# Involution on one Trainium2 core: GpSimd's ten taps move from the last to taps 7 to 16, and the logits are laid out pixel by pixel

## The chip, the cores and the metric

The program runs on one core of a Trainium2 chip. The metric is the device time of one execution in microseconds. The core has TensorE (matmuls, PE in the profile), VectorE (DVE), ScalarE (ACT), GpSimd (POOL) and SyncE (SP, which here only issues DMAs). Each engine runs its own list of instructions in order; they meet through semaphores.

## The reference, cut to what matters

A convolution-like layer (involution), then attention, then a routed feed-forward layer. The change touches the involution alone:

```
x1, x2, x3 = conv1x1(x, w1), conv1x1(x, w2), conv1x1(x, w3)       # 32, 32 and 256 channels, 56 x 56 pixels, 4 images
feat = concat([x1 - unfold_7x7(x2), p - unfold_7x7(p)])           # 49 taps per pixel, reflected borders
y = relu(bn(feat)); y = relu(bn(conv1x1(y, cw1)))
wgt = softmax(conv1x1(y, cw2, cb2), axis=taps)                    # 32 groups x 49 taps per pixel
out = sum over the 49 taps of  patch(x3, tap) * wgt[group, tap]   # 8 channels share a group
```

## The kernel before

The kernel has four stages, one after the other: projection (`project_stage`), involution (`conv_stage`), attention and feed-forward. The involution cuts the 56 rows of the image into 14 blocks of 4 rows. The 128 partitions are 4 images by 32 groups; a block has 224 pixels (`PW`).

For a block a there are two halves of work. The logits half: for each of the 7 rows i of the 7x7 window GpSimd forms `z(a, i)` = x1 - shifted x2 (7 taps at once), ScalarE applies a relu, and TensorE and ScalarE run the chain, two steps c per row i, 14 in all: `first` (matmul, cw1 and position features), `second` of ScalarE (relu), `second` of TensorE (matmul, cw2), `third` (ScalarE writes the logits `lg`). VectorE keeps a running maximum over taps (`rowmax`, L655) and folds it into `mx` (L659 to L665). The weighting half: GpSimd subtracts the maximum, row by row (`shift`, L466, `lg` to `ex`), ScalarE takes the exponent in place (`expo`, L548) and copies the weights of two taps to PSUM (`weights`) and into the products' ninth plane (`denominators`), VectorE multiplies two taps at once with the window of x3 (`pair`, L679), and TensorE adds the products of all taps into PSUM by an identity matmul (`add`, L742, nine planes: eight channels and the sum of the weights). The last ten taps (`OWN` = 10) are multiplied by GpSimd instead (`own`, L483), which also copies the weight into the ninth plane (L484). At the end VectorE divides (`divide`, L638 and L642) into `osb`, and SP stores `osb` to DRAM (`store`, L507).

The two halves of neighbouring blocks overlap. A slot handles the logits of block a and the weighting of block b = a - 1, in 20 units u, one per tap pair. The order on each engine is written out: `CH_AT` puts chain step c at unit c + 1, `MAX_AT` the maxima at units 5, 7, ... 17 (the fold at 17), `EXP_NEXT` and `FIRST_AT` the exponents of rows 2 to 6 and the relus, `OWN_AT` the units in which TensorE adds GpSimd's taps, and `POOL_ORDER` GpSimd's own sequence: z0, z1, shift 2, 3, z2, shift 4, 5, z3, shift 6, z4, z5, own 0, 1, z6, own 2 to 8; then shift 0 and shift 1 of the next block, then own 9. Shift 0 and 1 need the new `mx`, so they tie one slot to the next. VectorE divides block b - 1 in unit 1 of the slot.

The waits that matter here. `z(i)` needs the chain steps of row i - 2. SP issues the position features of row i after the chain steps of row i - 2 (four DMAs), and the store of block b - 1 right after those of row 3, so after chain step 3 (unit 4). GpSimd's taps alternate between two buffers: `own_a`, and `own_b`, which is the memory of `osb`; so `own(1)` waits until the store of the previous block has landed (L477). There are two product buffers, so pair p waits until pair p - 2 is summed.

## Time and profile before

| | us |
|---|---|
| median of 3 runs | 3883.24 (3878.19 to 3886.63) |
| the profiled execution's own time | 3877.12 |
| its span in the trace | 3875.3 |
| first and last division of the involution (starts) | 352.6 and 1714.1 |

The profile is one execution. A busy time is the union of an engine's instructions over the span or over a stretch. "Idle before" is the idle time of the engine just ahead of an instruction, with what ended it. PEclk is TensorE's granted clock as a share of the full 2.4 GHz. A matmul in float32 shows as two records, so one tap's 16 matmuls are 32 records.

### The profile page before, as it was taken

The numbers are of one execution on the slowest core, as the hardware profiler recorded it, in microseconds if no ns is written. First come the engines' busy times: TensorE is split into PE (matmuls) and PEld (weight loads), VectorE is DVE, ScalarE is ACT, GpSimd is POOL, SyncE is SP. The second block draws the span as 40 slices with busy tenths as digits, with TensorE's granted clock in tenths as the row PEclk, the third lists the DMA queues.
The fourth block names the chain that finished last, engine by engine and source line by source line (L and its number), as shares of the span: only waits on it lengthen the run. The fifth ranks groups of instructions, "written<-read, shape, count | busy, mean of one in ns | idle before, by whom it ended". The sixth has DMA issues, their size and how long they took to land. (4 is left out here: it accounts for less than half of the span.)

```text
span 3875.3 us, 102116 instructions
## 1 busy us (share of the span) xinstructions
PE 3125.9 (81%) x42750; PEld 1556.8 (40%) x42750; DVE 2569.3 (66%) x2229; ACT 2013.4 (52%) x3476; POOL 1962.9 (51%) x1032
## 2 busy tenths in 40 slices
PE   4767777878787777757989999999999994588797
PEld 1224444434343444324343524353344432355465
DVE  6259999999999999977456735664565545444212
ACT  1275556666666555524756575557556653334120
POOL 1269888988899898854140504051223401422422
PEclk9888899999999888888999999999999997788898
DMA  5611111111111111120121102111111103333443
GB/s 202 196 56 56 47 57 49 43 59 59 57 57 55 55 55 47 31 70 26 26 60 48 46 11 58 58 26 26 53 48 26 26 20 100 127 122 124 126 128 117
DMA packets 169451, 257.40 MB, mean 66 GB/s; under 512 B 81600, under 2 KB 128616, under 8 KB 165944
## 3 DMA queue, kind: packets, MB, share of 16 engines
q1 hardware_dynamic: 157120, 219.82, 18.8%
q0 software_dynamic: 11392, 31.02, 2.5%
q8 instruction: 359, 5.88, 0.6%
q14 instruction: 76, 0.62, 0.1%
q10 hardware_dynamic: 504, 0.05, 0.0%
HBM read 152.29 MB, written 79.27 MB: 60 GB/s over the span
## 5 line engine op out<-in xcount | busy, mean ns | idle before, releaser
L742 PE MATMUL ps<-prod,ident 32*32 32x504 f32 x17472 | 935.8, 646 | 257.2 <-issue 180.5
L679 DVE TENSOR_TENSOR prod<-ps,win 128x3584 f32<-128x3584 f32 x280 | 1054.5, 3790 | 99.7 <-PE ps L742 56.1
L1065 POOL TENSOR_TENSOR phk<-kv 128x768 f32<-128x768 f32 (+1 forms) x200 | 349.2, 1751 | 964.6 <-ACT kv L1173 902.6
L742 PEld LDWEIGHTS ps<-prod,ident 32*32 32x32 f32 x17472 | 380.5, 108 | 464.5 <-issue 413.9
L1217 ACT ACTIVATE phq<-ps 128x896 f32<-128x896 f32 x448 | 384.3, 917 | 212.7 <-PE ps L1501 211.8
L457 POOL TENSOR_TENSOR y<-a1w,x2w 128x1568 f32<-128x1568 f32 x98 | 345.9, 3538 | 137.5 <-PE ps L723 120.4
L466 POOL TENSOR_TENSOR ex<-lg,mx 128x1568 f32<-128x1568 f32 x98 | 345.1, 3541 | 16.0 <-DVE mx L665 15.8
L1501 PE MATMUL ps<-qst,sel 96*128 96x448 bf16 x1120 | 293.0, 365 | 25.1 <-ACT phq L1217 7.0
L561 ACT ACTIVATE ps<-ex 128x448 f32<-128x448 f32 x280 | 148.4, 533 | 293.9 <-DVE prod L679 293.9
L1316 DVE TENSOR_TENSOR phk<-ps,kv 128x1280 f32<-128x1280 f32 (+1 forms) x200 | 295.4, 1480 | 0.7 <-ACT ps L1177 0.7
L483 POOL TENSOR_TENSOR osb<-ex,win 128x1792 f32<-128x1792 f32 x70 | 270.2, 3859 | 28.5 <-PE ps L742 28.5
L483 POOL TENSOR_TENSOR own_a<-ex,win 128x1792 f32<-128x1792 f32 x70 | 262.3, 3747 | 43.4 <-issue 21.7
L585 ACT ACTIVATE y<-ps,u2c,s2c 128x784 f32<-128x784 f32 x189 | 189.1, 1000 | 169.2 <-PE ps L723 168.8
L1532 PE MATMUL ps<-phq,snt 128*32 128x448 f32 (+1 forms) x2240 | 273.2, 560 | 3.9 <-ACT phq L1219 3.9
L718 PE MATMUL ps<-y,cw1bd 32*32 32x392 f32 x3136 | 214.9, 514 | 52.1 <-DMA cwp<-cw1p 25.9
L1764 POOL DMA_INDIRECT yg<-rows_dram,dest x100 | 95.3, 953 | 313.2 <-DMA rows_dram<-yt 280.0
L2159 PE MATMUL ps<-xct,w_s 128*128 128x392 f32 x512 | 204.2, 547 | 61.6 <-ACT hid L1880 37.7
L1479 PE MATMUL ps<-phk,kv 128*32 128x288 f32 (+3 forms) x3200 | 237.4, 413 | 15.6 <-ACT phk L1182 9.0
L1458 PE MATMUL ps<-wkv_s,xn 128*128 128x256 f32 (+1 forms) x800 | 224.8, 406 | 9.5 <-ACT kv L1178 5.1
L592 ACT ACTIVATE lg<-ps,par 128x784 f32<-128x784 f32 x196 | 179.1, 914 | 81.6 <-PE ps L734 81.6
L1374 DVE TENSOR_TENSOR at<-ps,rd 128x448 f32<-128x448 f32 x56 | 35.0, 625 | 279.3 <-PE ps L1532 279.3
L734 PE MATMUL ps<-y,cw2bd 32*32 32x392 f32 x3024 | 191.8, 519 | 24.6 <-ACT y L585 21.4
(261 smaller groups left out, 5283.7 us busy)
## 6 DMA issues: line engine op xcount, KB each, us to landing
win<-planes SPq DMA_DIRECT2D x14, 2480.0 KB, 9.0
pf<-pf_dram SPq DMA_DIRECT2D x392, 55.1 KB
qst<-qsp SPq DMA_DIRECT2D x96, 196.0 KB, 4.7
planes<-stage SPq DMA_DIRECT2D x7, 1984.0 KB, 7.0
xs<-in_x SPq DMA_DIRECT2D x8, 1568.0 KB, 21.4
conv_dram<-osb SPq DMA_DIRECT2D x56, 224.0 KB, 4.8
t<-in_x SPq DMA_DIRECT2D x28, 448.0 KB, 4.0
xn<-conv_dram SPq DMA_DIRECT2D x28, 448.0 KB, 6.3
```

What stands on the lines that cost most here:

```text
L457: pool.tensor_tensor(o, x1, x2, ALU.subtract).then_inc(z_ready, 1)
L466: pool.tensor_tensor(ex[:, i], lg[:, i], m, ALU.subtract).then_inc(shifted, 1)
L483: pool.tensor_tensor(o[:, :, 0:SHARE], w.unsqueeze(2).broadcast_to([P, RW, SHARE, W]), xw, ALU.mult).then_inc(own_ready, 1)
L679: v.tensor_tensor(o, w, xw, ALU.mult).then_inc(prod_ready, 1)
L742: mm = pe.matmul(ps[32 * h:32 * h + 32, 4 + r, 0:DENC], diag(ident, r), x[32 * r:32 * r + 32, h].rearrange("p s w -> p (s w)"), start=begi ...
L1065: pool.tensor_tensor(phk[j % 2][0:r, :, ROT_V * DH:FLIN].rearrange("p h (r i) -> p h r i", i=DH), ki.unsqueeze(2).broadcast_to([r, HPG, RO ...
L1217: act.activation(dst, src, ACT.Square).then_inc(phq_done, 1)
L1316: v.tensor_tensor(phk[j % 2][0:r, :, DH:ROT_V * DH].rearrange("p h (r i) -> p h r i", i=DH), same.unsqueeze(2).broadcast_to([r, HPG, ROT_V ...
L1458: mm = pe.matmul(ps[0:r, 4 + j % 2, 0:HPG * DH + P], xn[:, k, j * P:j * P + r], wkv_s[:, k, hg, :], start=(k == 0), stop=(k == CH - 1))
L1479: pe.matmul(ps[DH * h:DH * h + DH, f, 0:hi - lo], kv[j % 3][0:r, v0:v0 + DH], phk[j % 2][0:r, h, lo:hi], start=(j == 0), stop=(j == NT - 1))
L1501: mm = pe.matmul(ps[:, h, 0:CT], sel[:, f, :], qst[:, h, ch(c)], start=True, stop=True)
L1532: mm = pe.matmul(ps[DH * h:DH * h + DH, out_bank(hg, c), 0:CT], snt[0:kr, f, DH * h:DH * h + DH], phq[k % 2][0:kr, h, :], start=(f == 0), ...
```

## The change

GpSimd's ten taps are no longer 39 to 48 but 7 to 16 (row 1 of the window and three of row 2), and they are spread over the slot instead of standing at its end. VectorE's pairs are formed of the remaining 39 taps. The denominator copy of GpSimd's taps goes to ScalarE. The logits and the running maximum are stored pixel by pixel, with the 7 taps of a window row next to each other: VectorE takes each row's maximum with a tensor_reduce over these 7 (instead of a running two-input maximum), and a second tensor_reduce over the 7 rows gives `mx` (instead of three folding steps). GpSimd's shift reads this layout and writes `ex` as before. Waits are made finer, the exponent of row 1 moves behind the first two `weights`, and the last of VectorE's pairs, not the last own tap, now ends the sum. In the projection stage two semaphores become one.

```diff
 OWN = 10
+OWN_TAPS = list(range(K7, K7 + OWN))
+PAIR_TAPS = [t for t in range(TAPS) if t not in OWN_TAPS]
...
-EXP_NOW = {FOLD_AT + 1: 0, FOLD_AT + 2: 1}
-EXP_NEXT = {2: 2, 4: 3, 6: 4, 8: 5, 10: 6}
-FIRST_AT = [0] + [2 * i - 1 for i in range(1, K7)]
-POOL_ORDER = [("z", 0), ("z", 1), ("shift", 2), ("shift", 3), ("z", 2), ("shift", 4), ("shift", 5), ("z", 3), ("shift", 6),
-              ("z", 4), ("z", 5), ("own", 0), ("own", 1), ("z", 6)] + [("own", k) for k in range(2, OWN - 1)]
-OWN_AT = [NPAIR_D - OWN + k for k in range(OWN)]
+EXP_FIRST_AT = FOLD_AT + 1
+EXP_NEXT = {0: 2, 2: 3, 5: 4, 8: 5, 11: 6}
+FIRST_AT = [2 * i for i in range(K7)]
+POOL_ORDER = [("z", 0), ("z", 1), ("shift", 2), ("shift", 3), ("own", 0), ("z", 2), ("own", 1), ("shift", 4), ("z", 3), ("own", 2),
+              ("shift", 5), ("z", 4), ("own", 3), ("shift", 6), ("own", 4), ("z", 5), ("own", 5), ("z", 6), ("own", 6), ("own", 7),
+              ("own", 8)]
+OWN_AT = [3, 5, 7, 9, 11, 13, 14, 15, 16, 18]
+def pairs_of_row(i):
+    return max([p // 2 + 1 for p, t in enumerate(PAIR_TAPS) if t // K7 == i], default=0)
+def own_to_row(i):
+    return sum(t // K7 <= i for t in OWN_TAPS)
...
-        lg = sb("lg", [P, K7, RW, K7, W])
+        lg = sb("lg", [P, K7, PW, K7])
-        run = sb("run", [P, RW, K7, W])
+        run = sb("run", [P, PW, K7])
...
             def shift(b, i):
                 pool.wait_ge(maxed, b.n + 1)
                 if not b.early(1):
-                    pool.wait_ge(den_in, NPAIR_D * (b.n - 1) + FREE_ROW_PAIRS if i < FREE_ROW else NPAIR_D * b.n)
-                if i == FREE_ROW and not b.early(1):
-                    pool.wait_ge(own_ready, 2 * OWN * b.n)
+                    if pairs_of_row(i):
+                        pool.wait_ge(den_in, NPAIR_D * (b.n - 1) + pairs_of_row(i))
+                    if own_to_row(i):
+                        pool.wait_ge(own_den, OWN * (b.n - 1) + own_to_row(i))
+                        pool.wait_ge(own_ready, OWN * (b.n - 1) + own_to_row(i))
+                l = lg[:, i].rearrange("p (h w) j -> p h j w", w=W)
-                pool.tensor_tensor(ex[:, i], lg[:, i], m, ALU.subtract).then_inc(shifted, 1)
+                pool.tensor_tensor(ex[:, i], l, m, ALU.subtract).then_inc(shifted, 1)
...
                 if k == 1 and not b.early(1):
                     pool.wait_ge(stored, 16 * RW * b.n)
-                if k >= 2:
-                    pool.wait_ge(own_used, (OWN - 1) * b.n + k - 1)
+                if k >= 2 or not b.early(1):
+                    pool.wait_ge(own_used, OWN * b.n + k - 1)
...
-                pool.tensor_copy(o[:, :, SHARE], w).then_inc(own_ready, 1)
...
                 if a:
                     shift(a, 0)
-                    shift(a, 1)
                 if b:
                     own(b, OWN - 1)
+                if a:
+                    shift(a, 1)
...
+            def own_denominators(b, k):
+                i, j = OWN_TAPS[k] // K7, OWN_TAPS[k] % K7
+                act.wait_ge(exped, b.q(i) + 1)
+                if k == 1 and not b.early(1):
+                    act.wait_ge(stored, 16 * RW * b.n)
+                if k >= 2 or not b.early(1):
+                    act.wait_ge(own_used, OWN * b.n + k - 1)
+                act.activation(own_buf[k % 2][:, :, SHARE], ex[:, i, :, j, :], ACT.Copy).then_inc(own_den, 1)
...
-                    act.activation(lg[:, i, h:h + 2].rearrange("p h j w -> p h (j w)"), ps[:, k:k + 2, 0:CW],
-                                   ACT.Identity, bias=par[:, CB2:CB2 + 1]).then_inc(logit, 1)
+                    act.activation(lg[:, i, h * W:(h + 2) * W].rearrange("p (h w) j -> p h j w", w=W),
+                                   ps[:, k:k + 2, 0:CW].rearrange("p h (j w) -> p h j w", w=W), ACT.Identity, bias=par[:, CB2:CB2 + 1]).then_inc(logit, 1)
...
-                    if a and u in EXP_NOW:
-                        expo(a, EXP_NOW[u])
+                    if a and u == EXP_FIRST_AT:
+                        expo(a, 0)
                     if a and u in FIRST_AT:
                         first(FIRST_AT.index(u))
+                    if b and u + 1 in OWN_AT:
+                        own_denominators(b, OWN_AT.index(u + 1))
                 if a:
                     weights(a, 0)
                     weights(a, 1)
                     denominators(a, 0)
+                    expo(a, 1)
...
-                    v.tensor_tensor(run[:], lg[:, i], lg[:, 0] if i == 1 else run[:], ALU.max).then_inc(ranmax, 1)
+                    v.tensor_reduce(run[:, :, i], lg[:, i], AX.X, ALU.max).then_inc(ranmax, 1)
...
-                    v.tensor_tensor(run[:, :, 0:3], run[:, :, 0:3], run[:, :, 4:7], ALU.max).then_inc(ranmax, 1)
-                    v.wait_ge(ranmax, NMAX * a.n + K7)
-                    v.tensor_tensor(run[:, :, 0:2], run[:, :, 0:2], run[:, :, 2:4], ALU.max).then_inc(ranmax, 1)
-                    v.wait_ge(ranmax, NMAX * a.n + K7 + 1)
+                    v.wait_ge(ranmax, K7 * (a.n + 1))
                     if b:
                         v.wait_ge(shifted, K7 * a.n)
-                    v.tensor_tensor(mx[:].rearrange("p (h w) -> p h w", w=W), run[:, :, 0], run[:, :, 1], ALU.max).then_inc(maxed, 1)
...
-                    await_ge(own_ready, 2 * (OWN * b.n + k + 1))
-                    mm = add(own_buf[k % 2], False, k == OWN - 1)
-                    if k < OWN - 1:
-                        mm.then_inc(own_used, 1)
-                    else:
-                        mm.then_inc(acc_done, 1)
+                    pe.wait_ge(own_den, OWN * b.n + k + 1)
+                    await_ge(own_ready, OWN * b.n + k + 1)
+                    add(own_buf[k % 2], False, False).then_inc(own_used, 1)
```

The waits of SP's `load_win` and of VectorE's `divide` on the end of the whole sum become waits on the last pair's sum.

## Rows read from the trace of the kernel before

**Rows 1.** Section 1 of the page: busy time of each engine, share of the span, instructions.
```profile
PE 3125.9 (81%) x42750; PEld 1556.8 (40%) x42750; DVE 2569.3 (66%) x2229; ACT 2013.4 (52%) x3476; POOL 1962.9 (51%) x1032
```

**Rows 2.** Busy time by stretch: one slot, mx to mx; columns in the first line.
```profile
core 0: us, PE busy (x) PEld busy (x) DVE busy (x) ACT busy (x) POOL busy (x), PEclk, DMA share, GB/s
...
549.80:656.10 106.30, 85.52 (x2128) 43.72 (x2128) 99.63 (x31) 64.77 (x82) 94.82 (x35) 0.92 0.18 54
```

**Rows 3.** The instruction that writes mx: count, ns min/median/max, first and last start.
```profile
L665 DVE TENSOR_TENSOR mx<-run x14: 391/393/440, 235.5 to 1617.6; 128x224 f32<-128x224 f32 x14
```

**Rows 4.** Groups of VectorE in that slot: busy us, mean ns, idle before.
```profile
L679 DVE TENSOR_TENSOR prod<-ps,win 128x3584 f32<-128x3584 f32 (+1 forms) x20 | 75.4, 3790 | 6.4 <-PE ps L742 3.3 <-ACT ps L561 2.9
L655 DVE TENSOR_TENSOR run<-lg,run 128x1568 f32<-128x1568 f32 x5 | 13.9, 2779 | 0.0
L661 DVE TENSOR_TENSOR run<-run 128x448 f32<-128x448 f32 x1 | 4.0, 3966 | 0.0
...
L659 DVE TENSOR_TENSOR run<-run 128x672 f32<-128x672 f32 x1 | 0.9, 907 | 0.0
```

**Rows 5.** The running maximum, all slots; then VectorE's timeline at the stage's end.
```profile
L655 DVE TENSOR_TENSOR run<-lg,run x70: 1773/2300/5244, 209.0 to 1609.9; 128x1568 f32<-128x1568 f32 x70
...
1714.07 1.56 DVE L638 RECIPROCAL run<-ps 128x224 f32<-128x224 f32 x1 [4.66 <-PE ps L742]
```

**Rows 6.** VectorE's reductions: ns min/median/max, elements out and in.
```profile
L1977 DVE TENSOR_REDUCE count<-mask x32: 543/544/547, 3263.1 to 3598.8; 128x15 f32<-128x375 bf16 x32
...
L1984 DVE TENSOR_REDUCE dig<-hits x32: 168/169/170, 3264.6 to 3601.6; 128x1 f32<-128x15 f32 x32
...
L1330 DVE TENSOR_REDUCE corr<-sn x8: 954/957/967, 1860.5 to 3109.1; 128x32 f32<-128x480 f32 x8
```

**Rows 7.** GpSimd's instructions by line: ns min/median/max.
```profile
L466 POOL TENSOR_TENSOR ex<-lg,mx x98: 3483/3539/3595, 236.0 to 1646.9; 128x1568 f32<-128x1568 f32 x98
...
L457 POOL TENSOR_TENSOR y<-a1w,x2w x98: 3222/3274/4403, 178.6 to 1581.3; 128x1568 f32<-128x1568 f32 x98
...
L483 POOL TENSOR_TENSOR own_a<-ex,win x70: 3689/3722/3895, 290.8 to 1704.6; 128x1792 f32<-128x1792 f32 x70
...
L484 POOL COPY own_a<-ex x70: 359/382/1962, 294.4 to 1708.3; 128x224 f32<-128x224 f32 x70
...
L168 POOL COPY stage<-stage x42: 317/483/491, 69.7 to 161.2; 128x72 f32<-128x72 f32 x42
...
L1041 POOL MEMSET eps<- x1: 117/117/117, 1726.8 to 1726.8; 128x1 f32 x1
```

**Rows 8.** Timelines of TensorE (chain step 3) and SP, and landing of one store.
```profile
587.79 0.81 PE L718 MATMUL ps<-y,cw1bd 32*32 32x392 f32 x9
...
588.44 0.40 PE L723 MATMUL ps<-pf,cwp 18*32 18x392 bf16 x8
...
589.03 3.19 SPq L535 DMA_DIRECT2D pf<-pf_dram  x4
592.49 4.12 SPq L507 DMA_DIRECT2D conv_dram<-osb  x4
...
DMA to landing us min/median/max: 3.7/4.8/5.7
```

**Rows 9.** Timeline of ScalarE in one unit; then its group of 224-element copies.
```profile
588.94 0.99 ACT L585 ACTIVATE y<-ps,u2c,s2c 128x784 f32<-128x784 f32 x1
...
591.34 0.91 ACT L592 ACTIVATE lg<-ps,par 128x784 f32<-128x784 f32 x1 [0.48 <-PE ps L734]
592.15 1.50 ACT L548 ACTIVATE ex<-ex 128x1568 f32<-128x1568 f32 x1
...
L568 ACT ACTIVATE prod<-ex 128x224 f32<-128x224 f32 x14 | 5.5, 391 | 42.2 <-PE ps L742 42.2
```

**Rows 10.** Timeline of TensorE: most of an own tap, and a gap.
```profile
619.13 1.37 PE L742 MATMUL ps<-own_a,ident 32*32 32x504 f32 x28
...
624.76 2.06 PE L742 MATMUL ps<-prod,ident 32*32 32x504 f32 x32 [3.25 <-issue]
```

More of the change, by code:

```diff
@@ L390, in conv_stage @@
         cwp = sb("cwp32", [P, REL], BF16)
-        run = sb("run", [P, RW, K7, W])
+        run = sb("run", [P, PW, K7])
         mx = sb("mx", [P, PW])
-        den = run[:].rearrange("p h j w -> p (h j w)")[:, 0:B * W].rearrange("p (b w) -> p b w", w=W)
+        den = run[:].rearrange("p x i -> p (x i)")[:, 0:B * W].rearrange("p (b w) -> p b w", w=W)
         cw1 = sb("cw1bd", [P, REL])
@@ L473, in own @@
                 pool.wait_ge(exped, b.q(i) + 1)
-                if k == 0 and not b.early(1):
-                    pool.wait_ge(acc_done, b.n)
                 if k == 1 and not b.early(1):
                     pool.wait_ge(stored, 16 * RW * b.n)
-                if k >= 2:
-                    pool.wait_ge(own_used, (OWN - 1) * b.n + k - 1)
+                if k >= 2 or not b.early(1):
+                    pool.wait_ge(own_used, OWN * b.n + k - 1)
                 w = ex[:, i, :, j, :]
@@ L517, in load_win @@
                 if not a.early(2):
-                    sp.wait_ge(acc_done, a.n - 1)
+                    sp.wait_ge(summed, NPAIR_D * (a.n - 1))
                 sp.dma_start(win[a.par][:], planes[:, bass.ds(a.n * RW, RW + K7 - 1)]).then_inc(win_in[a.par], 16)
@@ L551, in tap_pair @@
                 n = min(2, ND - 2 * p)
-                at = [t // K7 * K7 * PW + t % K7 * W for t in range(2 * p, 2 * p + n)]
+                at = [t // K7 * K7 * PW + t % K7 * W for t in PAIR_TAPS[2 * p:2 * p + n]]
                 e = ex[:]
@@ L636, in divide @@
                 acc = ps[:, 4:8]
-                v.wait_ge(acc_done, m + 1)
+                v.wait_ge(summed, NPAIR_D * (m + 1))
                 v.reciprocal(den, acc[:, :, SHARE * W:DENC]).then_inc(divided, 1)
@@ L647, in rowmax @@
                 def rowmax(i):
-                    if i == 0:
-                        return
                     v.wait_ge(logit, a.g(2 * i + 2))
-                    if i == 1 and b and not b.early(1):
+                    if i == 0 and b and not b.early(1):
                         v.wait_ge(divided, 2 * b.n)
-                    if i > 1:
-                        v.wait_ge(ranmax, NMAX * a.n + i - 1)
-                    v.tensor_tensor(run[:], lg[:, i], lg[:, 0] if i == 1 else run[:], ALU.max).then_inc(ranmax, 1)
+                    v.tensor_reduce(run[:, :, i], lg[:, i], AX.X, ALU.max).then_inc(ranmax, 1)
                 def fold():
-                    v.wait_ge(ranmax, NMAX * a.n + K7 - 1)
-                    v.tensor_tensor(run[:, :, 0:3], run[:, :, 0:3], run[:, :, 4:7], ALU.max).then_inc(ranmax, 1)
-                    v.wait_ge(ranmax, NMAX * a.n + K7)
-                    v.tensor_tensor(run[:, :, 0:2], run[:, :, 0:2], run[:, :, 2:4], ALU.max).then_inc(ranmax, 1)
-                    v.wait_ge(ranmax, NMAX * a.n + K7 + 1)
+                    v.wait_ge(ranmax, K7 * (a.n + 1))
                     if b:
                         v.wait_ge(shifted, K7 * a.n)
-                    v.tensor_tensor(mx[:].rearrange("p (h w) -> p h w", w=W), run[:, :, 0], run[:, :, 1], ALU.max).then_inc(maxed, 1)
+                    v.tensor_reduce(mx[:], run[:], AX.X, ALU.max).then_inc(maxed, 1)
                 def pair(p):
@@ L674, in pair @@
                     w = ps[:, 2 + p % 2, 0:n * PW].rearrange("p (n h w) -> p n h w", h=RW, w=W).unsqueeze(3).broadcast_to([P, n, RW, SHARE, W])
-                    at = [t // K7 * SHARE * WP + t % K7 for t in range(2 * p, 2 * p + n)]
+                    at = [t // K7 * SHARE * WP + t % K7 for t in PAIR_TAPS[2 * p:2 * p + n]]
                     x = win[b.par][:]
@@ L749, in pair @@
                         await_ge(prod_ready, NPAIR_D * b.n + p + 1)
-                    mm = add(prod[p % 2][:, k], p == 0 and k == 0, False)
+                    mm = add(prod[p % 2][:, k], p == 0 and k == 0, 2 * p + k == ND - 1)
                     if 2 * p + k == min(2 * p + 1, ND - 1):
```

21 lines of the change are left out of this document (7 added, 14 removed).

## The prediction

> **What bounds the kernel now.** I read the page first, then the involution stage slot by slot. The page's busy line [rows 1] has no engine over 81%, because it averages four stages. In a steady slot of the involution, 106.3 us [rows 2], VectorE is busy 94% (99.6 us), GpSimd 89%, TensorE 80%, ScalarE 61%. The slot period is the distance of two writes of mx: (1617.6 - 335.4) / 12 = 106.85 us for the twelve slots from block 1's mx to block 12's [rows 3]. A slot's VectorE work [rows 3, 4] is 20 tap pairs (75.4), six running maxima (five are 13.9, so 16.7), the fold (0.9 + 4.0 + 0.4), and some 3.5 of division. Of the 6.4 us idle ahead of the pairs, 2.9 are one wait for ScalarE's weights, ahead of pair 0; these weights stand behind the exponent of row 1, and that behind GpSimd's second shift. So VectorE bounds, and the joint between slots adds to it.
>
> Some of VectorE's time is not its own: the same running maximum takes between 1.77 and 5.24 us [rows 5].
>
> **The change, part by part.** Below, time 0 is the end of mx in a slot; S is the time of one GpSimd shift.
>
> Maxima on VectorE. Removed: 16.7 + 5.3 = 22.0 us a slot. Added: seven reductions of 1568 elements and one more for the fold. The trace has 375 elements in 544 ns and 15 in 169 ns [rows 6]: 1.04 ns each plus 153 ns, so 1.79 us, and eight make 14.3. The other end is the strided row, 480 elements in 957 ns, 2.0 ns each: 3.1 us, 25 in all. The new input lies together, so I take 1.79. VectorE's slot falls to 99.6 - 22.0 + 14.3 = 92 us; at the other end it is 103.
> The Trainium skill (VectorE: DVE Perf Modes, the table of ops and modes) says tensor_reduce has only the 1x mode and is the slowest op; the rows agree on 1x, which is all that a float32 two-input maximum had.
>
> GpSimd. Removed: ten copies of weights, 0.36 to 1.96 us each [rows 7], about 8.5 us a slot. Ten ScalarE copies of 224 elements come instead; ScalarE's copy of that size takes 0.39 [rows 9], so 3 to 4 us on an engine with 40 idle.
>
> The shifts. They now read the logits with 28 bytes between neighbours. No GpSimd row has a strided read alone. The one strided row is the copy of reflected columns, 72 single elements in 317 ns at least; the copy of 224 in runs of 56 takes 359, and a one-element MEMSET 117 [rows 7]. So (317 - 117) / 72 = 2.78 ns against 1.08: 1.7 ns more for a strided read and a strided write together. If the read has none of it, S stays 3.5; half gives 3.54 + 1568 x 0.85 ns = 4.9; all gives 6.2. I take 4.9, the even split, and keep 3.5 and 6.2.
> The Trainium skill (GPSIMD Engine Reference, Performance pitfalls for Q7 kernels) puts a read stepping over 8 bytes at about 2.9 cycles an element instead of 1.9; as an estimate from that page S would be 4.8. It speaks against this change, and no row here shows it alone.
>
> ScalarE's logits. The instruction reads PSUM in steps of 224 bytes. No ScalarE row has that. Ends: nothing, or doubled elements (+0.65 us each, about seven of them on the path below, +4.5 a slot). I take nothing.
>
> Stitching of slots. Weights of pair 0 and 1 now need row 0 only; the 2.9 us joint goes if mx comes in time. Late next: ScalarE's exponent of row 2 at unit 0, ahead of the relu of z(0).
>
> Own taps early. This decides. GpSimd's own(1) writes own_b, which is osb, and so waits for the store of the previous block. Before, own(1) stood behind z(5); now it stands behind z(2), ahead of own 2 to 8, shifts 4, 5, 6 and z(3) to z(6). ScalarE's denominator copy of own(1), at unit 4, has the same wait, ahead of second(4). SP issues that store only after the position features of row 3, and these wait for chain step 3. In the trace [rows 8]: step 3 ends on TensorE at 588.8, four feature DMAs are issued from 589.0 to 592.2, four stores from 592.5 to 596.6, and a store lands 3.7 to 5.7 us after its issue. The last is issued about 1 us before 596.6, so 7 + 4.8 = about 11.7 us from step 3 to the landing.
>
> **The loop from mx to mx, now through the store.** Durations start to start [rows 7 to 9]: own 3.66, z 3.24, relu or exponent 1.5, first half of a chain step on TensorE 1.06 (587.79 to 588.84), second on ScalarE 1.0, weights plus denominators 1.0 (588.94 to 591.34 is second, these two and 0.48 idle), third 0.9.
> 1. shift 0, own 9, shift 1, z0, z1, shift 2 on GpSimd, 3S + 10.1; exponent of row 2, relu of z(0), first chain step, hops: 4.2. Sum 3S + 14.3. (By then TensorE is through the division, at about 17 to 19.)
> 2. Steps 1 to 3. Unit 2 now holds exponent and relu together: 1.0 + 1.0 + 0.9 + 1.5 + 1.5 + 1.06; that is 7.0. The other two are 1.06 + 1.0 + 1.0 + 0.9 with a hop, 4.05 each. The three come to 15.1.
> 3. Store: 11.7.
> 4. GpSimd from own(1) to z(5): four owns, three z, three shifts: 24.4 + 3S.
> 5. ScalarE from z(5): relu, step 10, exponent of row 6, step 11, relu of z(6): 11.8.
> 6. Steps 12 and 13 and taps on TensorE until pair 14 is summed 7.8, pair 16 on VectorE 3.9, last maximum and fold 3.6: 15.3.
> 7. TensorE starves twice in this loop. After a gap of 3.25 us it came back slower, 32 records in 2.06 us where 28 took 1.37 [rows 10]. I put 2 us on the path.
>
> Sum: 14.3 + 15.1 + 11.7 + 24.4 + 11.8 + 15.3 + 2 = 94.6, + 6S. With S = 4.9 a slot is 124.0 us, 17.1 more than 106.85; twelve slots: +206. Block 0's slot has no store to wait for: GpSimd from mx to z(5) is six owns, six z and seven shifts, 75.7, + 11.8 + 15.3 = 102.8 against 335.4 - 235.5 = 99.9 [rows 3]: +3. The last slot has no chain: its joint (2.9) and most of the 4.7 us in which VectorE waited for the last own tap [rows 5] go, -7. Together +202: 3877.1 + 202 = 4079 beside the profiled execution, whose time is 6 us under the median of the runs; so 4085.
>
> What lies hidden: the ten ScalarE copies, VectorE's shorter work (92 in a slot of 124) and the copies taken from GpSimd (its sum is 93.6) all end in waiting. The merged semaphores of the first stage issue the same DMAs: nothing.
>
> **The rivals.**
> A. Same loop, strided reads free (S = 3.5): 94.6 + 21 = 115.6, +105, block 0's slot -5, tail -7: 3976. For it: the GpSimd operation has two inputs and may be bound elsewhere. Chance 0.2.
> B. Same loop, S = 6.2: 131.8 a slot, +299, +12, -7: 4187. Chance 0.17.
> C. The other side, faster: the store doesn't end last, because chain steps 0 to 3 run early or SP gets to it sooner. Then every slot is block 0's, 102.8 at S = 4.9: -49 + 3 - 7 = -53, 3830; with S = 3.5 VectorE's 92 or GpSimd's 84 decide and it goes to about 3720. It decides when the store lands before GpSimd reaches own(1), at 4S + 17 = 37 after mx; I have 56. Against it: SP's order is untouched and step 3 can't come before z(0) and z(1), which stand behind two shifts and own 9. Chance 0.08, and 0.03 that such gains and losses cancel within 0.2%.
> D. The change doesn't do what it says on VectorE: reductions at 2.0 ns an element. Only the last maximum and the fold lie on the loop, +2.7 a slot: 4117, inside the forecast's own range; it would decide only without the store.
> The Trainium skill (SBUF — State Buffer, on the shared port pair) says that VectorE with two SBUF inputs and GpSimd lock each other out for whole instructions, so one-input reductions would free both; the spread from 1.77 to 5.24 agrees. That is in the rows' uncontended times already.
>
> **How the numbers follow.** The forecast (S near 4.9, 4030 to 4140) has 0.52; A 0.2, B 0.17, C 0.08, even 0.03. The range 3945 to 4200 holds the forecast and A and B nearly whole. Faster by over 0.2% (what a measurement here can tell from no change): 0.08; within: 0.03; slower: 0.89.
>
> **What would show it.** In the profile after: GpSimd idle of some 15 to 20 us once a slot ahead of own(1), released by the DMA of conv_dram, and ScalarE idle ahead of its copy into own_b at the same time; shifts at 4.9 us; the reductions at 1.8; mx to mx at about 124; VectorE busy near 75% of a slot, waiting for TensorE and ScalarE. Wrong if GpSimd doesn't idle there, or if mx to mx is under 107.

## The result, and the profile after

| | before | after |
|---|---|---|
| median, us | 3883.23 (3878.19 to 3886.63, 4 runs) | 4208.01 (4204.82 to 4213.13, 4 runs) |
| ratio of the times, 95% interval | | 1.0834 [1.0819, 1.085] |
| profiled execution: time / span, us | 3877.12 / 3875.3 | 4213.13 / 4211.3 |
| end of mx of block 0, of block 1 | 235.9, 335.8 | 256.7, 374.2 |
| mean slot, mx of block 1 to mx of block 13 | 106.84 | 131.13 |
| last division starts; from there to the end | 1714.1; 2161.3 | 2039.7; 2171.6 |

The change is 8.3% slower; 4085 was forecast, and 4208 lies 8 us above the range. The 336 us between the two spans are made up of: block 0 before its mx +20.8, block 0's slot +17.6, twelve slots of +24.29 = +291.5, the end of the stage -4.3, everything after it +10.3. One of e1's two runs (5423 us, granted clock 0.55) and one of the kernel before beside it (4272 us, 0.72) are left out below.

First the page's busy line of after, beside [rows 1]:
```profile
PE 3231.2 (77%) x42750; PEld 1589.6 (38%) x42750; DVE 2482.7 (59%) x2215; ACT 2205.5 (52%) x3616; POOL 1887.4 (45%) x892
```
Then busy time by stretch in one of its slots, mx to mx, with the columns of [rows 2]:
```profile
767.70:899.90 132.20, 91.41 (x2128) 46.03 (x2128) 92.74 (x31) 78.53 (x92) 89.36 (x24) 0.86 0.15 44
```
VectorE did lose its 7 us of work (99.6 to 92.7) and GpSimd 5 (94.8 to 89.4), and neither shortens a slot of 132 in which no engine is busy for more than 71%. The groups of VectorE in that slot, against [rows 4]:
```profile
L688 DVE TENSOR_TENSOR prod<-ps,win 128x3584 f32<-128x3584 f32 (+1 forms) x21 | 79.6, 3800 | 39.3 <-PE ps L751 39.3
L668 DVE TENSOR_REDUCE run<-lg 128x224 f32<-128x1568 f32 x7 | 12.4, 1778 | 0.0
```
VectorE now waits 39.3 us in this slot for TensorE to free its product buffers, where it waited 3.3 for TensorE and 2.9 for ScalarE. The instruction that writes mx, against [rows 3]:
```profile
L674 DVE TENSOR_REDUCE mx<-run x14: 1786/1786/1787, 254.9 to 1946.0; 128x224 f32<-128x1568 f32 x14
```
The reductions take the 1.79 us forecast. Who holds the slot open shows in the timelines of that slot (start, duration, and in brackets the idle time before with its releaser): SP first:
```profile
816.57 3.19 SPq L541 DMA_DIRECT2D pf<-pf_dram  x4
820.02 4.14 SPq L513 DMA_DIRECT2D conv_dram<-osb  x4
```
Then GpSimd:
```profile
828.73 3.70 POOL L489 TENSOR_TENSOR osb<-ex,win 128x1792 f32<-128x1792 f32 x1 [24.32 <-DMA conv_dram<-osb]
832.39 4.34 POOL L475 TENSOR_TENSOR ex<-lg,mx 128x1568 f32<-128x1568 f32 x1
...
858.99 3.68 POOL L489 TENSOR_TENSOR own_a<-ex,win 128x1792 f32<-128x1792 f32 x1
862.63 3.28 POOL L463 TENSOR_TENSOR y<-a1w,x2w 128x1568 f32<-128x1568 f32 x1
```
GpSimd stands idle for 24.3 us ahead of own(1), released by the store of the block before, as forecast; the row of 862.63 is z(5), behind shift 6 and own(4). ScalarE over the same wait:
```profile
818.56 1.68 ACT L607 ACTIVATE lg<-ps,par 128x784 f32<-128x784 f32 x1 [0.20 <-PE ps L743]
820.03 1.52 ACT L589 ACTIVATE y<-y 128x1568 f32<-128x1568 f32 x1
828.68 0.39 ACT L583 ACTIVATE osb<-ex 128x224 f32<-128x224 f32 x1 [7.14 <-DMA conv_dram<-osb]
828.98 0.99 ACT L600 ACTIVATE y<-ps,u2c,s2c 128x784 f32<-128x784 f32 x1
...
836.75 1.51 ACT L554 ACTIVATE ex<-ex 128x1568 f32<-128x1568 f32 x1 [3.30 <-POOL ex L475]
```
The first row is what I had put at nothing: the logits write takes 1.68 us where it took 0.91 [rows 9]. The last is a second wait in the chain's way: the exponent of row 4 waits for shift 4, which now stands behind own(1), and ahead of the next chain steps. The page's groups of after over all slots (the last column is the idle time before them), beside [rows 7, 9]:
```profile
L475 POOL TENSOR_TENSOR ex<-lg,mx 128x1568 f32<-128x1568 f32 x98 | 423.0, 4325 | 62.5 <-DVE mx L674 62.5
L489 POOL TENSOR_TENSOR osb<-ex,win 128x1792 f32<-128x1792 f32 x70 | 260.2, 3717 | 396.8 <-DMA conv_dram<-osb 272.5
L607 ACT ACTIVATE lg<-ps,par 128x784 f32<-128x784 f32 x196 | 332.8, 1699 | 91.2 <-PE ps L743 91.2
```
The last division, in VectorE's timeline, beside [rows 5]:
```profile
2039.69 1.56 DVE L655 RECIPROCAL run<-ps 128x224 f32<-128x224 f32 x1 [2.61 <-PE ps L751]
```

### The profile page after: what moved, and what is told of

Its sections match the earlier page's. It is cut to its first block and busy times, and to the rows that moved or that the text cites. A ratio compares the mean times of both kernels' runs of the same rounds, so it can differ in the third digit from the quotient of the medians.

```text
span 4211.3 us, 102246 instructions
## 1 busy us (share of the span) xinstructions
PE 3231.2 (77%) x42750; PEld 1589.6 (38%) x42750; DVE 2482.7 (59%) x2215; ACT 2205.5 (52%) x3616; POOL 1887.4 (45%) x892
## 5 line engine op out<-in xcount | busy, mean ns | idle before, releaser
L751 PE MATMUL ps<-prod,ident 32*32 32x504 f32 x17472 | 1061.8, 708 | 161.4 <-DVE osb L659 72.5
L751 PEld LDWEIGHTS ps<-prod,ident 32*32 32x32 f32 x17472 | 427.3, 114 | 380.2 <-issue 332.2
L475 POOL TENSOR_TENSOR ex<-lg,mx 128x1568 f32<-128x1568 f32 x98 | 423.0, 4325 | 62.5 <-DVE mx L674 62.5
L489 POOL TENSOR_TENSOR osb<-ex,win 128x1792 f32<-128x1792 f32 x70 | 260.2, 3717 | 396.8 <-DMA conv_dram<-osb 272.5
L607 ACT ACTIVATE lg<-ps,par 128x784 f32<-128x784 f32 x196 | 332.8, 1699 | 91.2 <-PE ps L743 91.2
L463 POOL TENSOR_TENSOR y<-a1w,x2w 128x1568 f32<-128x1568 f32 x98 | 320.2, 3275 | 90.5 <-PE ps L732 73.7
L743 PE MATMUL ps<-y,cw2bd 32*32 32x392 f32 x3024 | 220.1, 592 | 104.1 <-ACT y L600 92.2
L727 PEld LDWEIGHTS ps<-y,cw1bd 32*32 32x32 f32 x3136 | 52.1, 110 | 483.9 <-issue 455.8
```

The lines of the kernel that those rows point to most:

```text
L463: pool.tensor_tensor(o, x1, x2, ALU.subtract).then_inc(z_ready, 1)
L475: pool.tensor_tensor(ex[:, i], l, m, ALU.subtract).then_inc(shifted, 1)
L489: pool.tensor_tensor(o[:, :, 0:SHARE], w.unsqueeze(2).broadcast_to([P, RW, SHARE, W]), xw, ALU.mult).then_inc(own_ready, 1)
L607: act.activation(lg[:, i, h * W:(h + 2) * W].rearrange("p (h w) j -> p h j w", w=W), ps[:, k:k + 2, 0:CW].rearrange("p h (j w) -> p h j w" ...
L751: mm = pe.matmul(ps[32 * h:32 * h + 32, 4 + r, 0:DENC], diag(ident, r), x[32 * r:32 * r + 32, h].rearrange("p s w -> p (s w)"), start=begi ...
```

## The experiments

"Slot" is the mean from block 1's mx to block 13's, from the trace. The kernels ran on several chips. On that of e5 to e8 the kernel before took 3795 us, against 3876 to 3883 on the others, and the traces there have some 85 us less after the last division (2077 to 2083). Matched instruction by instruction on VectorE, e7 stays within 4 us of before until some 1540 us behind that division, so the difference lies in the feed-forward stage. Kernels of different chips are therefore compared by ratio and slot, never by time.

| | what it is | time | ratio to before | mx of block 0 | slot |
|---|---|---|---|---|---|
| before | | 3883.2 | | 235.9 | 106.84 |
| after | | 4208.0 | 1.083 | 256.7 | 131.13 |
| e1_store_early | after, store issued earlier | 4114.7 (one run) | | 258.9 | 122.83 |
| e2_pixel_order | after, contiguous logits write | 4121.1 | 1.063 [1.060, 1.066] | 233.6 | 126.19 |
| e3_tap_major | after, old logits layout | 4070.6 | 1.050 [1.047, 1.053] | 237.5 | 122.03 |
| e4_tap_store | e3 and e1 | 3959.0 | 1.021 [1.018, 1.023] | 235.6 | 112.67 |
| e5_relu_order | e4 and new order of relus, exponents and GpSimd's list | 3785.7 | 0.997 [0.996, 0.998] | 236.0 | 105.81 |
| e6_layout_only | before, new layout | 3816.4 | 1.006 [1.004, 1.007] | 252.8 | 106.68 |
| e7_joint_only | before, new joint | 3810.3 | 1.004 [1.002, 1.006] | 235.1 | 108.46 |
| e8_pixel_all | e2, e1 and new order | 3727.3 | 0.981 [0.980, 0.983] | 234.8 | 101.92 |
| e9_late_store | e8 without e1 | 3948.1 | 1.018 [1.016, 1.021] | 235.4 | 112.48 |
| e10_strided_write | e8 without e2 | 3897.1 | 1.005 [1.003, 1.007] | 249.1 | 107.00 |
| e12_relu_only | after, new order alone | 4026.7 | 1.038 [1.036, 1.041] | 256.5 | 117.24 |
| e11_early_chain | e8, earlier chain | 3762.7 | 0.970 [0.968, 0.972] | 233.8 | 97.72 |

**e1_store_early.** SP issues the store ahead of the position features of row 2, so no longer behind chain step 3:
```diff
+                    if b and i == 2 and not b.early(1):
+                        store(b.n - 1)
...
-                    if b and i == 3 and not b.early(1):
-                        store(b.n - 1)
```


> The changed kernel with one move on SP: the store of block b - 1 is issued right after the window load, ahead of the position features of row 2, not behind those of row 3. Theory 1 (GpSimd and ScalarE wait for the store in every slot, and this wait is on the path from mx to mx): the changed kernel's slot of 131.1 us loses the 7.1 us in which ScalarE stood before its copy into own_b and the 3.3 us in which it then waited for shift 4, so about 120.7 a slot, total about 4208 - 125 = 4085; the 24 us of GpSimd idle ahead of own(1) is gone or small. Rival 2 (ScalarE's chain with its slower logits and new order sets the slot, the store's wait is hidden beside it): GpSimd's wait goes, but the slot stays at 131 and the total at 4208 within 10.

GpSimd's group for the odd own taps, all slots, no longer waits for the DMA:
```profile
L489 POOL TENSOR_TENSOR osb<-ex,win 128x1792 f32<-128x1792 f32 x70 | 259.9, 3713 | 224.7 <-PE ps L751 222.7 <-issue 2.0
```
own(1) starts 37.6 us after mx instead of 61.0, but a slot only falls from 131.1 to 122.8. The wait was real, and behind it another limit stood 8 us away: the chain itself. GpSimd now ends z(5) at 79.3 us after mx (mean of ten slots), and ScalarE comes to its relu only at 91.6; in after it was 97.3 and 99.6.

**e2_pixel_order.** The same elements, written in the order of memory. PSUM is now read in steps of 224 bytes, and SBUF is written without steps:
```diff
-  lg[...].rearrange("p (h w) j -> p h j w", w=W), ps[...].rearrange("p h (j w) -> p h j w", w=W)
+  lg[...].rearrange("p (h w) j -> p h w j", w=W), ps[...].rearrange("p h (j w) -> p h w j", w=W)
```


> The changed kernel, but ScalarE's logits instruction runs pixel by pixel: it reads PSUM in steps of 224 bytes and writes its output in order; the changed kernel reads in order and writes in steps of 28 bytes. Same data, same layout. If the strided write costs the 0.79 us (0.91 to 1.70 an instruction), the instruction is back at about 0.92, thirteen of them on the slot's loop give 10 us a slot, and the total is about 4208 - 12 x 10 - 21 = 4065. If a step on either side costs the same, it stays at 1.7 and the total at 4208 within 10.

```profile
803.43 0.91 ACT L607 ACTIVATE lg<-ps,par 128x784 f32<-128x784 f32 x1 [0.20 <-PE ps L743]
```
The write is back at 0.91. So the step on the PSUM side costs ScalarE nothing, and the 28-byte step of the write costs 0.79 us, 1.0 ns an element. A slot falls by 4.9, half of what I expected: I had multiplied by nearly every write of a slot. That the others fall into time in which the path waits for the store or for GpSimd is an inference; 4.9 / 0.79 makes about six writes on the path. Block 0's mx falls by 23.1, which is 1.65 for each of 14 steps, twice the price of the write. Busy time by stretch of block 0's chain, the same 50 us, first of after and then of e2 (the third number from the right is the granted clock):
```profile
180.00:230.00 50.00, 28.52 (x384) 9.65 (x384) 7.15 (x4) 31.82 (x25) 20.17 (x7) 0.57 0.22 78
```
```profile
180.00:230.00 50.00, 26.48 (x560) 10.60 (x560) 10.75 (x7) 34.82 (x36) 21.93 (x7) 0.91 0.28 98
```
TensorE's timeline of after in that stretch:
```profile
210.76 1.56 PE L727 MATMUL ps<-y,cw1bd 32*32 32x392 f32 x16 [2.03 <-ACT lg L607]
```
With the longer write TensorE sat idle 2 us before each batch of first matmuls (1.3 to 1.5 in e2), and its granted clock in this stretch was 0.57, near the lower level of 1.2 GHz, where it was 0.91 with the short one, near 2.4. In 50 us it issued 384 matmul records instead of 560. The trace of e10, which has the long write too, shows both levels in this chain and so prices the two apart. Busy time by stretch, first three steps, then one:
```profile
204.60:216.40 11.80, 5.75 (x120) 2.22 (x120) 3.58 (x2) 10.23 (x9) 4.42 (x2) 0.93 0.06 19
216.40:221.60 5.20, 3.19 (x40) 1.05 (x40) 0.00 (x0) 2.66 (x2) 2.07 (x1) 0.50 0.14 47
```
A step takes 3.9 us at 0.93 and 5.2 at 0.50; with the short write it takes 3.1 at 1.00 (e2). So the write adds the 0.79 of its own length to each step, 11 of the 23 us, and the other 12 are the lower clock: in after ten of the steps take 5.0 to 5.3. That share varies: e10 and e12 run this chain alike, on one chip, and reach block 0's mx at 249.1 and 256.5. No run tells why the clock stays low for longer in one than in the other.

**e3_tap_major.** The logits and their shift as before the change; the maxima read across 224 bytes:
```diff
-        lg = sb("lg", [P, K7, PW, K7])
+        lg = sb("lg", [P, K7, RW, K7, W])
...
-                    v.tensor_reduce(run[:, :, i], lg[:, i], AX.X, ALU.max)
+                    v.tensor_reduce(run[...], lg[:, i].rearrange("p h j w -> p h w j"), AX.X, ALU.max)
```


> The changed kernel's schedule with the logits laid out as in the kernel before (tap by tap): ScalarE writes them in order, GpSimd's shift reads them in order, and VectorE's seven reductions read them in steps of 224 bytes. Theory 1: ScalarE's instruction 0.91, shift 3.5, reduction about 3.1 (the strided row of the kernel before, 2.0 ns an element). Of the loop 13 x 0.79 + 6 x 0.78 go and one slower maximum (1.3) comes: about 117.5 a slot, total about 4208 - 163 - 25 = 4020. The store's wait stays, some 20 us of GpSimd idle a slot. Rival 2 (only ScalarE's chain counts): 121 a slot, 4060.

Its reductions between 700 and 1500 us:
```profile
L668 DVE TENSOR_REDUCE run<-lg 128x224 f32<-128x1568 f32 x45 | 140.8, 3129 | 0.0
```
The strided reduction costs 3.13, the upper end of my bounds [rows 6], and the layout as a whole (logits write +0.79, shift +0.79, six reductions inside a waiting VectorE) costs a slot 9.1 us more than the old one with its slower reductions. I expected 13.6; 122.0 is nearer to the rival's 121.

**e4_tap_store.** e3 with the edit of e1.

> Both: logits tap by tap and the store moved ahead of the features of row 2. Theory 1: 117.5 less about 10 a slot, so 107 to 108, total about 3900, within 1% of the kernel before. Rival 2 (the store's wait is hidden): no faster than the kernel with the layout alone, 4020 to 4060.

A slot of 112.7, +5.8 on before, where I expected 107 to 108: neither the late store nor the new layout is left, and it is still slower. Relu i stands in unit 2i, at the end of the unit just ahead of the one with its chain step, and behind an exponent in units 0, 2 and 8. What ended TensorE's idle time ahead of the first matmuls between 400 and 1600 us (us, times):
```profile
  ACT y L589: 144.9, 74
```
That is every even step (148 steps fall into the window). Before the change that row is missing; in after it is 183.8, 65. Steps 0 to 13 take 74.6 us here and 65.4 before the change.

**e5_relu_order.** e4 with the relus a unit earlier, the exponents of rows 4 and 6 moved by one unit, so that only unit 0 still holds both, and GpSimd's list in matching places: shift 4 ahead of own(1), z(4) ahead of shift 5, z(5) ahead of shift 6, z(6) ahead of own(4):
```diff
-EXP_NEXT = {0: 2, 2: 3, 5: 4, 8: 5, 11: 6}
-FIRST_AT = [2 * i for i in range(K7)]
-POOL_ORDER: ... ("z", 2), ("own", 1), ("shift", 4), ("z", 3), ("own", 2), ("shift", 5), ("z", 4), ("own", 3), ("shift", 6), ("own", 4), ("z", 5), ...
-OWN_AT = [3, 5, 7, 9, 11, 13, 14, 15, 16, 18]
+EXP_NEXT = {0: 2, 2: 3, 6: 4, 8: 5, 10: 6}
+FIRST_AT = [0] + [2 * i - 1 for i in range(1, K7)]
+POOL_ORDER: ... ("z", 2), ("shift", 4), ("own", 1), ("z", 3), ("own", 2), ("z", 4), ("shift", 5), ("own", 3), ("z", 5), ("shift", 6), ("z", 6), ("own", 4), ...
+OWN_AT = [3, 5, 7, 9, 12, 13, 14, 15, 16, 18]
```


> The kernel with logits tap by tap and the early store (112.7 us a slot), with the relu of row i at unit 2i - 1 as in the kernel before (not 2i), the exponents at units 0, 2, 6, 8, 10, and GpSimd's list reordered so that each z comes in time (own taps 3 to 9 later). Theory 3 (what is left of the loss is that each relu is issued one unit ahead of its chain step, twice behind an exponent, so that TensorE waits for it at every second step): steps 0 to 13 took 74.6 us there and 65.4 in the kernel before; some 7 of the 9 come back, 105 to 106 a slot, total about 3875. Rival (VectorE's slower reductions, 3.14 each, or GpSimd's sum bound it): no more than 2 us a slot, 3935.

The slot falls by 6.9, below that of before, and the relu row of e4 falls to 16.3 us: with the old layout the spread of the own taps pays, by 0.3%.

**e6_layout_only.** Before, with the pixel layout alone: `lg`, `run`, the logits write, the shift's read and the reductions as in the change:
```diff
-        lg = sb("lg", [P, K7, RW, K7, W])
+        lg = sb("lg", [P, K7, PW, K7])
...
-                    v.tensor_tensor(run[:], lg[:, i], lg[:, 0] if i == 1 else run[:], ALU.max)
+                    v.tensor_reduce(run[:, :, i], lg[:, i], AX.X, ALU.max)
```

> The kernel before with the layout of the change alone: logits written pixel by pixel (ScalarE 0.91 to 1.70), reductions on VectorE, strided shifts (4.32). Schedule, taps and waits as before. If ScalarE and the chain set the pace (thirteen steps at 0.79 more, partly beside VectorE's waits), about 113 a slot and mx of block 0 some 20 us later: total about 3877 + 75 + 20 + 8 = 3980. If VectorE's relief (22 to 14.3 us) decides, about 100 a slot and 3815.

I expected 2.7% and got 0.6%: slots are the same (106.7), only block 0 is longer (+17 to its mx). Busy time by stretch, over the length of a slot, and VectorE's pairs in it:
```profile
708.00:815.00 107.00, 82.93 (x2138) 39.91 (x2115) 92.27 (x30) 74.90 (x82) 92.53 (x35) 0.94 0.18 54
```
```profile
L672 DVE TENSOR_TENSOR prod<-ps,win 128x3584 f32<-128x3584 f32 (+1 forms) x20 | 75.8, 3793 | 14.5 <-PE ps L735 7.7 <-ACT ps L562 6.7
```
ScalarE's busy time went from 64.8 to 74.9 [rows 2]. Equal slots don't mean that this cost nothing. VectorE has 7 us less work (92.3 for 99.6) and idles 8 us more ahead of its pairs (14.5 for 6.4 [rows 4]). Over ten slots the first chain step reaches ScalarE 29.7 us after mx (26.1 before), behind three longer shifts (2.5 of it), and the last at 96.1 (91.3 before). So the chain ends 4.8 us later, and VectorE's shorter work takes that up. Of the 4.8 only 1.2 lie between the first and the last step: there the longer writes do fall mostly into ScalarE's idle time.

**e7_joint_only.** Before, with the exponent of row 1 behind the first two `weights`, and own 9 ahead of shift 1:
```diff
-EXP_NOW = {FOLD_AT + 1: 0, FOLD_AT + 2: 1}
+EXP_NOW = {FOLD_AT + 1: 0}
...
                 if a:
                     shift(a, 0)
-                    shift(a, 1)
                 if b:
                     own(b, OWN - 1)
+                if a:
+                    shift(a, 1)
```


> The kernel before with the joint of the change alone: GpSimd's last own tap stands between shift 0 and shift 1, and the exponent of row 1 behind the first weights. Pair 0 then waits for the exponent of row 0 alone. The 2.9 us idle ahead of pair 0 goes: about 104 a slot, total about 3877 - 13 x 2.9 = 3840. Rival: VectorE, earlier by 2.9, then waits for TensorE or ScalarE in units 2 to 6 instead, and nothing is gained.

No gain but a loss of 0.4%. The 2.9 us of the joint do go (VectorE's waits for ScalarE's weights fall from 42.9 us over all slots to 5.8), and come back in the running maximum. Its first instruction in each slot, duration in ns min/median/max; before the change it was 1791/2830/2946:
```profile
L656 DVE TENSOR_TENSOR run<-lg x14: 1793/7208/8268, 202.0 to 1570.9; 128x1568 f32<-128x1568 f32 x14
```
The timelines of VectorE and then of GpSimd in one slot:
```profile
814.15 7.21 DVE L656 TENSOR_TENSOR run<-lg 128x1568 f32<-128x1568 f32 x1
```
```profile
802.70 7.07 POOL L466 TENSOR_TENSOR ex<-lg,mx 128x1568 f32<-128x1568 f32 x2
809.70 3.29 POOL L457 TENSOR_TENSOR y<-a1w,x2w 128x1568 f32<-128x1568 f32 x1
812.92 3.56 POOL L466 TENSOR_TENSOR ex<-lg,mx 128x1568 f32<-128x1568 f32 x1
816.42 3.28 POOL L457 TENSOR_TENSOR y<-a1w,x2w 128x1568 f32<-128x1568 f32 x1
```
The maximum takes 1.77 us undisturbed [rows 5] and 7.21 here; it ends 1.7 us after GpSimd's run of back-to-back instructions does. The mean of all six maxima rose from 2.68 to 3.34, 4 us a slot. The Trainium skill (SBUF — State Buffer, on the shared port pair) has VectorE with two SBUF inputs and a GpSimd instruction that reads SBUF lock each other out for whole instructions. This trace agrees, and shows that one wait can outlast more than one of them: the maximum of 814.15 sits out the rest of the shift and the whole z behind it. The one-input reductions of rows that lie together take 1.77 to 1.79 in every trace here.

**e8_pixel_all.** After with the edits of e1, e2 and e5.

> The changed kernel with its three losses mended at once: ScalarE's logits pixel by pixel but written in order (0.91), early store, relus and GpSimd's list as in the run beside it. VectorE has 92 us a slot, GpSimd 90, chain steps as in the kernel before. If the theory of three separate losses holds, 100 to 103 a slot, total about 3877 + 10 - 12 x 5 = 3815 to 3840, faster than both. If strided shifts (4.32) make z late, about 106 and 3880.

Faster than both kernels, 0.981: slots of 101.9, 3.9 less than e5 with the old layout. Busy time by stretch, one slot:
```profile
740.20:842.00 101.80, 84.75 (x2128) 44.23 (x2128) 92.04 (x31) 67.89 (x92) 89.59 (x24) 0.90 0.19 57
```
And GpSimd's timeline in it, shift 4 and own(1), which no longer waits:
```profile
776.80 4.38 POOL L475 TENSOR_TENSOR ex<-lg,mx 128x1568 f32<-128x1568 f32 x1
781.14 3.72 POOL L489 TENSOR_TENSOR osb<-ex,win 128x1792 f32<-128x1792 f32 x1
```

The next three take e8 apart again: the store and the write each with and without the other, and the order with both losses in place.

**e9_late_store.** e8, with the store back behind the features of row 3 (the diff of e1, reversed).

> The fastest kernel so far (pixel order everywhere, joint writes, relus and exponents in order, store issued before the features of row 3) with one edit: the store is put back behind the features of row 3, as in the changed kernel. Theory (the store sits on the loop's path because own tap 1 reuses the buffer that the store reads): chain step 3 ends some 43 us after mx, the store lands some 12 us later, own tap 1 starts at 55 instead of 41, and a slot takes 107 to 109 us instead of 101.9: about 70 us more in all. Rival (the store's wait was hidden behind GpSimd's own work anyway): own tap 1 still starts by 45 and the time does not move by more than 10 us.

```profile
836.62 3.70 POOL L489 TENSOR_TENSOR osb<-ex,win 128x1792 f32<-128x1792 f32 x1 [13.34 <-DMA conv_dram<-osb]
```
Chain step 3 ends 43.1 us after mx, own(1) starts at 54.4 instead of 40.9, and the slot grows by 10.6: place as expected, size over three more than the expected 5 to 7. own(1) starts 13.5 later and the slot ends 10.6 later, so the chain behind it makes up only 3 of them.

**e10_strided_write.** e8, with the old write order (the diff of e2, reversed).

> The fastest kernel so far with one edit: ScalarE writes its logits in tap-major places, in steps of 28 bytes, as the changed kernel does, while PSUM is read in the same order of memory as there. Theory (each such write takes 1.70 us instead of 0.92 and ScalarE sets the pace of the chain): chain steps of about 5.1 us, the last step at 95 to 97 us after mx instead of 91, a slot of 107 to 109 us, about 90 us more in all with the 20 us of the first maxima. Rival (VectorE or TensorE sets the pace and the longer write fills ScalarE's idle time): a slot under 104 us.

Steps of 5.15 us, the last at 96.9 after mx, a slot of 107.0 and +14 to block 0's mx: ScalarE's pace sets the chain here, as the theory had it. Ahead of the first matmuls between 400 and 1600 us TensorE waits for the logits write, which it doesn't do once in e8 (us, times):
```profile
  ACT lg L607: 45.1, 51
```

**e12_relu_only.** After, with the order of e5 alone.

> The changed kernel with the order of relus, exponents and GpSimd's list of the fastest kernel, and nothing else: the store stays late, the logits are still written in steps of 28 bytes. Theory (relus that wait behind exponents and long logits writes stretch chain steps 1 to 3 and 9 to 12): own tap 1 starts some 58 us after mx instead of 61, a slot takes 113 to 116 us instead of 131, about 4010 us in all. Rival (only the store and the size of the logits write count): a slot within 3 us of 131.

A slot of 117.2, 13.9 less than after, 1.2 over the upper end that I expected; own(1) starts at 57.0. The largest of the three parts is thus the one that no step of the prediction priced by itself. As means of ten slots, after and then e12: chain step 3 reaches ScalarE at 48.4 and 44.6; from there to own(1) 11.7 and 12.0; from own(1) to the end of z(5) 37.2 and 25.0; from there to the relu of z(6) 14.7 and 13.0; to the next mx 19.1 and 22.7. So 12.2 of the 13.9 lie in GpSimd's list behind own(1), where the new order has shift 4, shift 6 and own(4) no longer between own(1) and z(5): 2 x 4.32 + 3.66 = 12.3. Busy time by stretch, one slot of e10, then of e12:
```profile
780.40:888.10 107.70, 84.39 (x2128) 40.88 (x2128) 92.18 (x32) 77.62 (x92) 89.63 (x24) 0.92 0.18 54
```
```profile
827.80:945.50 117.70, 87.31 (x2128) 41.58 (x2128) 92.39 (x32) 77.75 (x92) 89.59 (x24) 0.87 0.16 49
```
Same work on ScalarE, VectorE and GpSimd to 0.2 us; TensorE at the lower clock is busy 2.9 us longer. They are 10 us apart, and what differs is idle time. With the new order the slot as a function of the other two is:

| slot, us | store late | store early |
|---|---|---|
| write in 28-byte steps | 117.24 (e12) | 107.00 (e10) |
| write in memory's order | 112.48 (e9) | 101.92 (e8) |

The store is worth 10.2 and 10.6, the write 4.8 and 5.1: with this order they add up. Beside the change's own order the store is worth 8.3 (e1) and the write 4.9 (e2).

**e11_early_chain.** e8, with z made earlier on GpSimd, the relu of row 0 ahead of the exponent of row 2, the exponents of rows 5 and 6 and the units of GpSimd's taps on TensorE one or two later:
```diff
-EXP_NEXT = {0: 2, 2: 3, 6: 4, 8: 5, 10: 6}
-OWN_AT = [3, 5, 7, 9, 12, 13, 14, 15, 16, 18]
+EXP_NEXT = {0: 2, 2: 3, 6: 4, 9: 5, 12: 6}
+OWN_AT = [4, 6, 8, 10, 13, 14, 15, 16, 17, 18]
...
-POOL_ORDER = [("z", 0), ("z", 1), ("shift", 2), ("shift", 3), ("own", 0), ("z", 2), ("shift", 4), ("own", 1), ("z", 3), ("own", 2), ("z", 4), ("shift", 5), ("own", 3), ("z", 5), ("shift", 6), ("z", 6), ...
+POOL_ORDER = [("z", 0), ("shift", 2), ("z", 1), ("shift", 3), ("z", 2), ("own", 0), ("z", 3), ("shift", 4), ("own", 1), ("z", 4), ("own", 2), ("z", 5), ("shift", 5), ("own", 3), ("z", 6), ("shift", 6), ...
+                    if a and u == 0:
+                        first(0)
                     if b and u in EXP_NEXT:
                         expo(b, EXP_NEXT[u])
...
-                    if a and u in FIRST_AT:
+                    if a and u in FIRST_AT[1:]:
                         first(FIRST_AT.index(u))
```


> The fastest kernel so far with the start of a slot in another order: GpSimd makes z of row 0, then shift 2, z of row 1, shift 3 and z of row 2 before its first own tap, and ScalarE writes the relu of row 0 ahead of the exponent of row 2. Theory (the chain waits at its start for shift 2 behind two z): chain step 0 ends 18 to 22 us after mx instead of 28.5, a slot takes 96 to 98 us, some 50 to 60 us less in all. Rival (GpSimd's 90 us of work a slot and the buffers of its own taps set the end): the slot stays at 100 to 102 us.

The fastest kernel here, 0.970 [0.968, 0.972]. Chain step 0 ends at 24.6 instead of 28.5, later than the 18 to 22 expected, and the slot is 97.7, inside what was expected. Which of the moves gave the 4.2 us was not tried. Busy time by stretch, one slot:
```profile
716.00:814.60 98.60, 83.17 (x2128) 44.67 (x2128) 92.24 (x32) 67.68 (x92) 89.74 (x25) 0.93 0.20 59
```
And VectorE's group of pairs in it:
```profile
L690 DVE TENSOR_TENSOR prod<-ps,win 128x3584 f32<-128x3584 f32 (+1 forms) x21 | 79.6, 3797 | 6.1 <-PE ps L753 6.0
```
VectorE is busy 94% of it and idles 6 us instead of after's 39. That is its share and its idle time in the kernel before [rows 2, 4], in a slot shorter by the 7 us of work that the change takes from it: the gain that the change's parts hold once nothing else is late.

## Why the prediction was off

**The miss, term by term.** Forecast and measured, between the profiled executions: block 0 up to its mx 0 and +20.8; block 0's slot +3 and +17.6; twelve slots +206 and +291.5; the end of the stage -7 and -4.3; the rest 0 and +10.3. That makes +202 and +336. Of these 134 us of difference 11 are not in the medians, since the profiled execution was 6 under the median before and 5 over it after; 4208 is 123 over 4085.

**Right.** The direction, and the mechanism with its place: own(1) waits for the store of the block before, behind chain step 3 and the four feature DMAs; ScalarE waits at the same time. From step 3 to own(1) 11.7 was forecast and 12.4 came; from own(1) to z(5), 24.4 + 3 x 4.32 = 37.4 by the formula, 37.1 came (ScalarE, delayed too, took z(5) up 2.7 later, 868.59 against 865.91). Reductions 1.79: exact. The shift at 4.32 lies between rival A's and the forecast's, and excludes B. Rivals C and D fell: the store did end last in after (e1 moves own(1) by 23 us), and no reduction took 2.0 ns an element except in e3, where the input is strided. The tail was -4.3 for -7. Two slips of the working: rival A's block 0 slot is -7 by its own lists, not -5 (102.8 - 7 x 1.4 = 93.0 against 99.9), and the range ends 13 us above rival B's 4187, so it never held B nearly whole.

**Too high: S.** I took 4.9 us for a shift with a 28-byte read; it is 4.32 in after, so a strided read costs this two-input operation 0.79 us, 0.5 ns an element. With that the sum gives 94.6 + 25.9 = 120.5 a slot. The 3.5 us too many hid as much of the terms below in each slot, 42 us in all; that the result came as near to the range as 8 us is luck.

**The first step that failed: ScalarE's logits, "I take nothing".** It failed twice. I misread the code: both sides are arranged as p, h, j, w, so the instruction reads PSUM in order and writes SBUF in steps of 28 bytes (e2, which has the pattern that I priced, shows that it would indeed have been free). I took that end without giving a reason. And the price: my other end, +0.65 us on about seven writes of the path, +4.5 a slot, was nearly right; measured are +0.79 and 4.9 a slot (e2), 59 us over twelve slots. I had that number and took the other end.

**A term left out: block 0's chain.** The sum began at block 0's mx. Ahead of it, 14 chain steps with nothing else to do carry every longer write (11 us) and the lower clock (the rest of the +20.8); e2 takes all of it away. Block 0's slot, +3 forecast, was +17.6, 117.5 us: I let GpSimd's list bound it, and the chain did. With no store to wait for it is 117.5 in e1 too, 107.5 with the short write (e2) and 103.5 with the new order (e12), near my 102.8.

**The second, and somewhat larger: steps 2, 5 and 6 of the loop, mis-sized.** In the slot shown, the legs against the sum at S = 4.32 are 28.1 for 27.3; 20.5 for 15.1; 12.4 for 11.7; 37.1 for 37.4; 15.8 for 11.8; 18.3 for 15.3, with 2.0 for the clock beside them: 132.2 for 120.6. Legs 2, 5 and 6 hold 12.4 of it, the long write included: with the short one (e2) they are 1.9, 2.8 and 0.5 shorter, as means of ten slots. That leaves some 7 us that are not the write's. I priced the chain as durations laid end to end, with the relu beside its exponent only in unit 2. e4 shows the stretched steps without the late store and the new layout: TensorE waits for a relu at every even one. The new order of e12 takes 3.8 of it out up to chain step 3. Leg 6 stays unexplained: no run takes it apart. Had I taken the write at +4.5, the sum at S = 4.32 would be 125.0, still 6 short of 131.1.

**Right, and not followed up: leg 4.** Of the 13.9 us a slot that e12 gives back, 12.2 are inside what I had priced right, z(5) behind own(4) and three shifts. I computed that leg and never asked what another order of the same list would give.

**Against before**, step by step: e8 is 4.9 a slot under it; the long write adds 5.1 (e10), the late store 10.2 (e12), the change's own order 13.9 (after), together 24.3. These are differences along one row of kernels, so they add up by construction; taken off after first, the store is worth 8.3 (e1) and the write 4.9 (e2).

**Open.** The 10 us behind the last division are not in the changed stage: all kernels with the change, but for those of the chip of e5 to e8, show them or part of them (2166 to 2172 against 2161). Matched on VectorE, after is within 1.5 us of before up to 1540 us behind that division and 9.5 later at 1850, so they come in the routed feed-forward stage; no run tells why. How the 13.9 us of the order divide between relus, exponents and GpSimd's list was not tried.

## What to carry to other kernels

Lay a loop through every engine's list, not only through the engine with the new wait: an instruction in an in-order list that waits (ScalarE's copy into own_b, its exponent for a late shift) delays all behind it, and moving work early is only as good as the buffer it lands in. When an access pattern changes, write down for each operand which side has the step before pricing it, and when only a bound has a price, price the whole chain at that end too, also in the first block where nothing hides it. A part can look free because another pays for it: in e6 the slot stayed the same while the chain ended 4.8 us later, and VectorE's 7 us less of work went into that. The same long write costs 5 us a slot where nothing hides it (e10). So look at the idle times too when a total doesn't move.
